# Segment sums of a graph network on one core: unread products on TensorE, VectorE's operands in PSUM

## The reference

```python
def _sage_conv(h, src, dst, W_self, W_neigh, b):
    msg_sum = jax.ops.segment_sum(h[src], dst, num_segments=N_NODES)
    deg = jax.ops.segment_sum(jnp.ones_like(dst, dtype=h.dtype), dst, num_segments=N_NODES)
    h_neigh = msg_sum / jnp.maximum(deg, 1.0)[:, None]
    return h @ W_self + h_neigh @ W_neigh + b          # three layers: sage0, sage1, sage2
...
    msg = xt[row] * alpha[..., None]                   # attention over incoming edges: gat
    out = jax.ops.segment_sum(msg, col, num_segments=n)
...
    def f(y):                                          # called four times: rk0 to rk3
        return jax.ops.segment_sum(y[src3] * e3, dst3, num_segments=N)
...
    msg = h_all[src, etypes] * norm                    # a matrix per relation: rel
    agg = jax.ops.segment_sum(msg, dst, num_segments=x.shape[0])
```

## Time and profile before

| | |
|---|---|
| Median of 3 runs | 21,753.78 us (21,741.98 to 21,762.46) |
| Profiled execution | 21,875.38 us, its span 21,873.6 us |
[...]
| Busy: PE, PEld, DVE, ACT, POOL | 47%, 33%, 29%, 12%, 65% of the span |

### The profile page before, as it was taken

One profiled execution on the slowest core, in us unless ns is written; L12 is line 12 of the kernel. 1 busy time (PEld: TensorE's weight loads), 2 busy tenths in 40 slices (PEclk: granted clock), 3 DMA queues, 4 the chain that ended last, 5 costly groups with the idle time before them and its releaser, 6 DMA issues.

```text
span 21873.6 us, 147184 instructions
## 1 busy us (share of the span) xinstructions
PE 10234.6 (47%) x41175; PEld 7163.9 (33%) x41176; DVE 6368.7 (29%) x12754; ACT 2697.4 (12%) x4406; POOL 14143.2 (65%) x14027
## 2 busy tenths in 40 slices
PE   5214444444477634434444444444444344448744
PEld 2113333333222323323333333333333333334333
DVE  8401111111477632222222222222222222226422
ACT  0001101010155421101000011001011001100010
POOL 5876676766755676676666666666666666660365
PEclk8655555555688755555555556555555565658855
DMA  1111211211100011121212112121211212125412
GB/s 31 9 23 46 46 42 46 42 46 47 13 1 1 2 14 46 46 48 46 45 47 43 51 46 46 46 48 46 46 47 46 48 46 46 46 46 211 188 46 45
DMA packets 555319, 1025.63 MB, mean 47 GB/s; under 512 B 276823, under 2 KB 344031, under 8 KB 529110
## 3 DMA queue, kind: packets, MB, share of 16 engines
q0 software_dynamic: 448640, 761.10, 16.4%
q1 hardware_dynamic: 102595, 256.61, 3.1%
q10 hardware_dynamic: 3600, 1.51, 0.0%
HBM read 767.92 MB, written 248.53 MB: 46 GB/s over the span
## 4 chain that ended last, share of the span: by engine, by line
POOL 35%; another core or an unknown queue 20%; issue 20%; PE 12%; DVE 7%; DMA 3%; ACT 2%; DVEq 1%; ACTq 0%; POOLq 0%; SPq 0%
POOL rows L405 28%; POOL list_f L389 5%; PE ps L1011 4%; PE ps L1101 3%; POOL list_r L389 3%; ACT work L462 2%; PE ps L1055 2%; DMA rows<-table,rows_F 1%; DVE onehot L701 1%; DVE rows L715 1%; DVE peak_tile L816 1%; DMA rows<-table,rows_R 1%; PE ps L1052 1%; PE ps L1017 0%
## 5 line engine op out<-in xcount | busy, mean ns | idle before, releaser
L1011 PE MATMUL ps<-rows,onehot 128*128 128x128 f32 (+1 forms) x22880 | 5352.9, 406 | 8395.6 <-DVE rows L715 4747.5
L405 POOL DMA_INDIRECT rows<-table,rows_F x7040 | 6864.8, 975 | 3332.5 <-issue 2028.8
L1011 PEld LDWEIGHTS ps<-rows,onehot 128*128 128x128 f32 x22880 | 4677.5, 299 | 9555.0 <-issue 7950.5
L405 POOL DMA_INDIRECT rows<-table,rows_R x3520 | 3419.8, 972 | 1630.1 <-issue 995.5
L462 ACT COPY work<-ps 128x1188 f32 x1430 | 1641.9, 1148 | 16874.2 <-remote 9132.3
L701 DVE TENSOR_TENSOR onehot<-iota,list_F 128x512 f32<-128x512 f32 x1980 | 1284.5, 690 | 5973.0 <-ACT work L462 3385.1
L1000 PE MATMUL ps<-naught 128*128 128x396 bf16 x4290 | 1592.9, 505 | 1492.3 <-issue 1491.9
L405 POOL DMA_INDIRECT rows<-rel_table,rows_F x880 | 851.6, 968 | 1261.1 <-DMA rel_table<-list_R 856.3
L389 POOL DMA_INDIRECT list_f<-list_F,work x850 | 1064.6, 1252 | 401.6 <-issue 258.7
L413 POOL DMA_INDIRECT rows<-peak_table,rows_F x880 | 831.3, 945 | 761.7 <-PE ps L1055 534.4
L389 POOL DMA_INDIRECT list_r<-list_R,rows_R x850 | 1110.6, 1307 | 259.0 <-issue 259.0
(11 more groups left out here) (198 smaller groups left out, 6211.3 us busy)
## 6 DMA issues: line engine op xcount, KB each, us to landing
rel_table<-list_R SPq DMA_DIRECT2D x196, 1024.0 KB, 3.9
rows<-table,rows_F POOLq DMA_INDIRECT x7040
rows<-table,rows_R POOLq DMA_INDIRECT x3520
table<-H SPq DMA_DIRECT2D x5, 3136.0 KB
rows<-peak_table,rows_F POOLq DMA_INDIRECT x880
rows<-rel_table,rows_F POOLq DMA_INDIRECT x880
list_f<-list_F,work POOLq DMA_INDIRECT x850
list_r<-list_R,rows_R POOLq DMA_INDIRECT x850
```

The source lines that it names most:

```text
L405: pool.indirect_dma_start(out=rows[:, t % UNROLL, 0:FEAT], out_offset=None, in_=from_table, in_offset=bass.IndirectOffsetOnAxis(ap=rows_of ...
L1011: ins = mm(into, onehot[:, s, :], rows[:, s, 0:width], start=False, stop=True, skip_group_check=True)
```

## The change

TensorE's two extra jobs in a window go to VectorE. `clear_half` writes the zeros by a memset, and `add_first` adds the running sums of the first block to the half in PSUM; ScalarE now waits for `window_added`, which add_first reports. VectorE's compare reads `iota_ps`, a copy of iota in PSUM bank 6, and its scaling reads the weights from the same bank, copied there for 96 tiles at a time. Behind each quad TensorE issues four products of the identity with itself, 128x512 in fp32, into bank 7, which nothing reads (`keep_clock`). In the unscaled passes TensorE waits for both membership matrices of a window at once.

```diff
+IDLE_PRODUCTS = 4
...
+CHUNK = (512 - P) // HEADS
...
+        iota_ps = ps[:, 6, 0:P]
+        weights_ps = ps[:, 6, P:]
...
+        def weights_of(name):
+            L = lists[name[-1]]
+            return share if name == "gat F" else L[:, :, 7:8] if name == "rel F" else L[:, :, 3:3 + HEADS]
...
-                    act.wait_ge(window_summed, m0 + w + 1)
+                    act.wait_ge(window_added, m0 + w + 1)
...
-            def block_sums(name, weights=None, aux=None):
-                L = lists[name[-1]]
+            def block_sums(name, aux=False):
+                key, L = name[-1], lists[name[-1]]
                 n0, m0 = quads_before(name), windows_before(name)
-                def members_of_window(w):
+                width = AUX if aux or name == "sage0 F" else FEAT
+                def clear_half(w):
                     if m0 + w >= 2:
                         dve.wait_ge(window_stored, m0 + w - 1)
+                    v.memset(half_of[w % 2][:, :, 0:SLOTS * AUX // SLOT_BANKS], 0.0)
+                def members_of_window(w):
                     for q in (2 * w, 2 * w + 1):
                         slots = slice(q % QRING * QUAD, (q % QRING + 1) * QUAD)
-                        v.tensor_tensor(onehot[:, slots, :], iota[:, :].unsqueeze(1).to_broadcast([P, QUAD, P]),
+                        v.tensor_tensor(onehot[:, slots, :], iota_ps.unsqueeze(1).to_broadcast([P, QUAD, P]),
                                         L[:, q * QUAD:(q + 1) * QUAD, 2].unsqueeze(2).to_broadcast([P, QUAD, P]),
                                         ALU.is_equal).then_inc(quad_members, 1)
                 def scale_quad(q):
-                    slots, tiles = slice(q % QRING * QUAD, (q % QRING + 1) * QUAD), slice(q * QUAD, (q + 1) * QUAD)
+                    at, words = q * QUAD % CHUNK, 1 if name == "rel F" else HEADS
+                    if at == 0:
+                        n = min(CHUNK, TILES - q * QUAD)
+                        if q:
+                            dve.wait_ge(quad_scaled, n0 - quads_before(SCALED[0]) + q)
+                        st(v.tensor_copy(weights_ps[:, 0:n * words].rearrange("p (t h) -> p t h", h=words), weights_of(name)[:, q * QUAD:q * QUAD + n, :]))
+                    weights = weights_ps[:, at * words:(at + QUAD) * words].rearrange("p (t h) -> p t h", h=words)
+                    slots = slice(q % QRING * QUAD, (q % QRING + 1) * QUAD)
                     dve.wait_ge(quad_landed[name][q % QRING], 16 * QUAD * (q // QRING + 1))
-                    if aux is not None:
-                        st(move(rows[:, slots, FEAT:AUX], aux[:, tiles, :]), False)
-                    at = rows[:, slots, 0:FEAT]
-                    if weights is None:
-                        v.tensor_tensor(at, at, L[:, tiles, 7].unsqueeze(2).to_broadcast([P, QUAD, FEAT]), ALU.mult).then_inc(quad_scaled, 1)
-                    else:
-                        at = at.rearrange("p t (h c) -> p t h c", c=HC)
-                        v.tensor_tensor(at, at, weights[:, tiles, :].unsqueeze(3).to_broadcast([P, QUAD, HEADS, HC]), ALU.mult).then_inc(quad_scaled, 1)
-                v.memset(SUM_OF[name[-1]][:, 0, :], 0.0).then_inc(sums_clear, 1)
+                    if aux:
+                        st(move(rows[:, slots, FEAT:AUX], weights), False)
+                    here = rows[:, slots, 0:FEAT].rearrange("p t (h c) -> p t h c", h=words)
+                    v.tensor_tensor(here, here, weights.unsqueeze(3).to_broadcast([P, QUAD, words, FEAT // words]), ALU.mult).then_inc(quad_scaled, 1)
+                firsts = []
+                def add_first(w):
+                    if w % 10 == 0:
+                        firsts[:] = firsts_of(mybir.EngineType.DVE, key, w, 10)
+                    dve.wait_ge(quad_summed, n0 + 2 * w + 2)
+                    if m0 + w:
+                        dve.wait_ge(window_stored, m0 + w)
+                    half = half_of[w % 2][:, 0, 0:width]
+                    v.tensor_tensor(half, half, sums_flat[key][:, bass.ds(firsts[w % 10], width)], ALU.add).then_inc(window_added, 1)
+                st(v.memset(SUM_OF[key][:, 0, :], 0.0))
+                st(v.tensor_copy(iota_ps, iota[:, :]))
+                clear_half(0)
                 members_of_window(0)
                 for w in range(WINDOWS):
                     if name in SCALED:
                         scale_quad(2 * w)
+                    if w:
+                        add_first(w - 1)
+                    if name not in SCALED and w + 1 < WINDOWS:
+                        clear_half(w + 1)
                     if w + 1 < WINDOWS:
                         members_of_window(w + 1)
                     if name in SCALED:
                         scale_quad(2 * w + 1)
+                        if w + 1 < WINDOWS:
+                            clear_half(w + 1)
+                add_first(WINDOWS - 1)
...
+            def keep_clock():
+                for _ in range(IDLE_PRODUCTS):
+                    mm(ps[:, 7, :].rearrange("p (a b) -> p a b", a=4), ident[:, :], ident[:, :].unsqueeze(1).to_broadcast([P, 4, P]), start=True, stop=True)
             def block_sums(name, width=FEAT):
-                key, n0, m0 = name[-1], quads_before(name), windows_before(name)
-                pe.wait_ge(sums_clear, SUMS.index(name) + 1)
+                key, n0 = name[-1], quads_before(name)
                 for w in range(WINDOWS):
-                    if w % 2 == 0:
-                        firsts = firsts_of(mybir.EngineType.PE, key, w, 2)
                     slots = slots_of(mybir.EngineType.PE, key, w)
                     half = half_of[w % 2].rearrange("p k f -> p (k f)")
-                    cleared = SLOTS * AUX // SLOT_BANKS
-                    for k in range(SLOT_BANKS):
-                        mm(half_of[w % 2][:, k, 0:cleared].rearrange("p (a b) -> p a b", a=4), naught[:, :],
-                           naught[:, 0:cleared // 4].unsqueeze(1).to_broadcast([P, 4, cleared // 4]), start=True, stop=True)
                     for j in range(WINDOW):
                         q, s = 2 * w + j // QUAD, (w * WINDOW + j) % UNROLL
                         if j % QUAD == 0:
                             if name in SCALED:
                                 pe.wait_ge(quad_scaled, n0 - quads_before(SCALED[0]) + q + 1)
                             else:
-                                pe.wait_ge(quad_members, n0 + q + 1)
+                                if j == 0:
+                                    pe.wait_ge(quad_members, n0 + q + 2)
                                 pe.wait_ge(quad_landed[name][q % QRING], 16 * QUAD * (q // QRING + 1))
                         into = half[:, 0:width] if j == 0 else half[:, bass.ds(slots[j - 1], width)]
                         ins = mm(into, onehot[:, s, :], rows[:, s, 0:width], start=False, stop=True, skip_group_check=True)
                         if j % QUAD == QUAD - 1:
                             ins.then_inc(quad_summed, 1)
-                    if m0 + w:
-                        pe.wait_ge(window_stored, m0 + w)
-                    mm(half[:, 0:width], ident[:, :], sums_flat[key][:, bass.ds(firsts[w % 2], width)],
-                       start=False, stop=True, skip_group_check=True).then_inc(window_summed, 1)
+                            keep_clock()
             def turn(dst_bank, of, j):
                 return tr(ps[:, dst_bank + j // 4, (j % 4) * P:(j % 4 + 1) * P], of, ident[:, :])
```

More of the change, by code:

```diff
@@ L553, in _ @@
             v.memset(zeros[:, :], 0.0).then_inc(consts, 1)
-            v.memset(naught[:, :], 0.0).then_inc(consts, 1)
             st(v.tensor_scalar(valid[:, :], part[:, :], float(LAST), None, ALU.is_lt), False)
@@ L860, in _ @@
             dve.wait_ge(shares_exp, ITERS + 1)
-            block_sums("gat F", weights=share, aux=share)
+            block_sums("gat F", aux=True)
             st(v.tensor_scalar(REC[:, :, :], ACC[:, :, FEAT:AUX], 1e-16, None, ALU.add))
@@ L882, in _ @@
                         name_rows("R", 0)
-                    attr = lists[key][:, :, 3:3 + HEADS]
-                    block_sums(f"rk{k} {key}", weights=attr, aux=attr if k == 0 else None)
+                    block_sums(f"rk{k} {key}", aux=k == 0)
                 n = AUX if k == 0 else FEAT
```

6 lines of the change are left out of this document (2 added, 4 removed).

## The result

The changed kernel took 21,860.72 us (median of 5 runs, 21,841.7 to 21,869.27), the kernel before 21,752.14 us (5 runs, 21,719.23 to 21,762.46). The ratio is 1.0051, with a 95% interval of 1.0036 to 1.0066: slower, by 108.6 us in the medians. The forecast of 19,730 us and its whole range were missed.

The account below looks back on a forecast made before the run. POOL's gathers were taken as the bound, with 2,051 us of excess from late completions and long gathers; 21,875 - 2,051 + 26 = 19,850, less 122 for plain runs, gave 19,730 us, range 19,620 to 20,450.

Parts of the forecast that it names:

- What bounds the kernel: Thirteen gather passes: POOL's undisturbed pitch is 1.248 us a gather, and the passes last 2,051 us longer than POOL needs.
- late completions: POOL's waits before gathers for TensorE and "remote": 1,687 us beyond ordinary issue gaps, with TensorE some 9 us late in one stretch.
- long gathers: Gathers in the passes running over 0.944 us, beginning under VectorE instructions that read two SBUF tensors: 335 us.
- unread products: Four TensorE products behind each quad keep the clock full and remove the late completions: 1,687 us, bounds 0 to 1,687.
- rival 2: Late completions stay, coming of something other than TensorE's idleness or clock: 21,417 us if all, 20,570 if half; chance 0.12.
- VectorE's operands in PSUM: Compares and scalings read one SBUF tensor instead of two, so long gathers end: 335 us taken, bounds 0 and 335.
- VectorE's new work: Clear, add, compares and scalings per window on VectorE: 4.5 us of a 9.98 us window, hidden under POOL.
- Clears and first block off TensorE: L1000 and L1017 leave TensorE; beside POOL's time, so worth nothing alone, but they make room for the products.
- The sum: Whole execution: 21,875 - 2,051 + 26 = 19,850 us, less 122 gives 19,730; everything outside the 13 passes stays.
- The correction of -122 us: Whole execution: the median of plain runs, 21,753.8 us, lies 121.6 us below the profiled one, so 122 is subtracted.
- the edges: Per pass, an iota copy, one clear and the last products: at most 3.45 us; 2 us allowed, 26 us in all.
- Rival 3: TensorE becomes the bound at every quad, slower than before, if the granted clock does not rise under the products; chance 0.05.

Follow-up runs that it names:

- chip C: Chip of the third group of follow-up runs; the kernel before takes 19,808 us there, and the changed kernel without products 19,671.43 us.
- chip D: Chip of the fourth group of follow-up runs; the kernel before takes 21,892 us there, and the changed kernel 22,016.21 us.
- paced: Changed kernel with a POOL IOTA behind each gather, waiting for the IOTA before it: 19,803.05 us (ratio 1.001) and 19,832.61 us (1.0012) on chips A and C.
- half-size kernels: Changed kernel gathering 64 rows instead of 128 (19,157.61 and 19,153.53 us), or 64 words a row instead of 128 (19,631.91 and 19,637.13), on chips A and C.
- chips A and C: Chips of the first and third groups of follow-up runs; the kernel before takes 19,784 and 19,808 us there.
- chip B: Chip of the second group of follow-up runs; the kernel before takes 21,907.84 us there, and the changed kernel 22,028.66 us.
- group 2: Runs on chip B: kernel before 21,907.84 us, changed kernel 22,028.66, changed kernel with operands in SBUF 22,166.67, kernel before with products alone 22,115.6.

## Why the prediction was wrong

*What bounds the kernel* was read rightly: POOL's gathers at 1.248 us, and an excess of 2,051 us made of late completions and long gathers. On chip C, where the late completions are missing, the passes do last 1,101 us.

*The step that failed* is the one on the unread products: "This part is what I expect to take the late completions away: they come with a mostly idle TensorE at the low clock". In the rows that is 561.28 of 1255 us busy at a granted 0.57. The step took a thing seen beside the waits for their cause. The evidence was a correlation within one trace, between stretches which differ in more than TensorE's activity: at L1101 no gather runs at all (POOL is busy 0.00 us in the earlier trace rows). Four cells now separate the two. Clock low and TensorE mostly idle (without products, the pass rk1 F): late on chip D (450.06 of 1249 us busy at a granted 0.51), on time on chip C (449.95 of 1101 at 0.50). Clock high and TensorE nearly full: late in the changed kernel (1063.73 of 1257 at 0.91, 2264.0 us remote), on time in the paced and the half-size kernels on chips A and C (90 to 94% busy at 0.99 to 1.00, no wait named remote). The late completions follow the chip, not the clock. The prediction's own sign for this step, waits of 4 us at a high clock, has come. Of the 1,687 us nothing was gained; rival 2's mechanism held whole. Its price, 21,417, was missed too, by 444 us: it still counted 335 us for the operands and nothing for the products. The lesson in the working is the 1,687 against its own lower bound of 0: the rows could not choose between the ends, and the forecast put 0.72 on the upper one.

*The products also cost*, which the sum had at nothing. Alone they cost 211.0 us on chip B; beside the rest of the change they cost 22,016.21 - 21,807.61 = 208.6 us on chip D. There POOL's waits for "remote" and TensorE are 2377.9 + 15.0 us with products and 2081.1 + 101.8 without, 210.0 apart, so the cost is waiting of POOL. On chip C, with completions on time, they cost nothing that shows. That they fit beside POOL was worked out rightly: a quad's products and sum take TensorE an estimated 3.45 + 0.86 = 4.31 us of POOL's 4.99 (from the earlier trace rows and 1.248 us a gather, as in group 2), and the quads in the timeline follow each other every 4.33 us (12136.48, 12140.81), at a granted 1.00 there. But the room was counted against a steady 4.99 us a quad. After each hold TensorE has queued quads to catch up on, and 3.6 us of products stand ahead of every one of them. In the kernel without products the 16 matmuls of two quads run in one go after a hold, in 3.94 us at a granted 0.55, 1.97 us a quad; with them each quad takes its 4.33. That this is how the 209 us arise is argued from the rows; no run tried a number of products between 0 and 4.

*VectorE's operands in PSUM* did what the prediction said to the gathers: 339.8 us of POOL time gone for the 335 forecast, and 810 back when the operands go back in the changed kernel. The term that failed is their worth in time: 335 was taken, and they are worth 138.0 and 140.3 us by the runs on chips B and D. On the chips with late completions part of POOL's saving is waited away again. On chips A and C the whole change without products gains 129 and 136 us, also far under 335; no trace of the kernel before was taken there, so how much of that is long gathers stays open. The longest gather is 986 ns with one SBUF operand in VectorE's compares and scalings, and 2667 ns with two (the kernel with SBUF operands on chip D, below, with one long gather under two compares). Which part of a gather is held, the runs do not tell.

```profile
1608.70 1.27 DVE L712 TENSOR_TENSOR onehot<-iota,list_F 128x512 f32<-128x512 f32 x2
1608.71 1.47 POOL L412 DMA_INDIRECT rows<-table,rows_F  x1 [0.30 <-issue]
```

```profile
L412 POOL DMA_INDIRECT rows<-table,rows_F x7040: 940/947/2667, 1482.1 to 18671.6; - x196
```

*VectorE's new work* was sized well or too high, and stayed hidden:

```profile
L741 DVE TENSOR_TENSOR ps<-ps,work 128x128 f32<-128x128 f32 (+1 forms) x1430 | 427.4, 299 | 7773.8 <-remote 7351.5
L729 DVE TENSOR_TENSOR rows<-rows,ps 128x512 f32<-128x512 f32 x2200 | 1495.2, 680 | 2025.1 <-DMA rows<-table,rows_F 876.8
L706 DVE MEMSET ps<- 128x1188 f32 x1430 | 1498.6, 1048 | 788.6 <-issue 498.5
```

The clear takes 1.05 us (1.40 taken, 1.0 the other end; the copy's row gives 1.33 in proportion, not 1.40), the add 0.30 (0.29), the scaling 0.68 (0.70). The 7,351.5 us that add_first waits for "remote" are the late completions again, now on VectorE.

*Clears and first block off TensorE*, together with the operands, are the rest. Without products the change is faster than before by 84 us on chip D (21,891.96 - 21,807.61) and by 129 to 136 us on chips A and C. Since the operands give 140.3 us on chip D, the moved clears and sums and the new waits would cost 56 us there, if the parts add up; that part was not run alone.

*The sum*, put right for chip D: operands -140, products +209, the rest +56 by difference, in all the measured +124. The correction of -122 us from profiled to plain time was also no property of the kernel: on chip B a profiled execution of before had a span of 21,891.5 us, below the 21,907.84 of its plain runs. The 3.45 us that bound the edges in the prediction are the estimate from the earlier trace rows given in group 2; no run had the edges alone.

Rival 3 (TensorE the bound for want of clock) did not happen: the granted 0.91 is above 4.31 / 4.99 = 0.86, the share at which TensorE's work on a quad would last as long as POOL's (an estimate, if that work goes with the clock). Nor did its sign, a TensorE without idle time and a wait of POOL at every quad: POOL waited for "remote" or TensorE before 854 of 11,440 gathers, and there are 2,860 quads.

What stays open is the cause of the late completions. It is not the clock, not TensorE's idleness, not the slot registers, not the gathers' rows. Nor do the gathered rows land late: VectorE's scaling starts 2.53 us after the start of the quad's last gather in the late stretch (12130.94, 12133.47) and on chip C alike (11021.03, 11023.56). The waits come in a rhythm. On chip D 715 gathers of the changed kernel wait for "remote" and 659 without products. POOL's waits of over 1.5 us for "remote" or TensorE stand there 23 us apart with products (679 of 811 distances), and without them most often 33 to 34 us (328 of 663). Where products are queued a wait ends in matmuls some 0.70 us apart. No row of the trace names what holds them. The unaltered changed kernel never ran on a chip with completions on time, and the kernel before was not traced on one, so that the chips differ by their completions is shown for the variants that ran on both kinds.

## What to carry to other kernels

A wait that the trace lays to "remote" has no cause in it; a forecast that rests on removing it should keep its price at both ends and give the lower end real weight, until an experiment has moved the wait. Filling TensorE to 86% of its period (an estimated 4.31 of 4.99 us a quad) was free on the chip where the work arrived evenly (passes of 1,100 us with products and half-width gathers, 1,101 without products), and cost some 210 us where it was held up: there, as argued above, the filler stands ahead of the catching up. And compare only with the kernel before on the same chip: here chips differed by 10%, twenty times the effect.

The version to keep is the changed kernel with IDLE_PRODUCTS = 0. It was faster than before on both kinds of chip: 0.9932 (0.9915 to 0.9948), 0.9931 (0.9915 to 0.9948) and 0.9968 (0.9956 to 0.9979).

## What the runs showed of the hardware

Chips of one type ran one program in two times: the kernel before at 19,784 and 19,808 us on two of them, and at 21,752 to 21,905 us in the other four results. For the kernel without products, traced on both kinds, 1,937 of the 2,136 us between chips D and C lie in the gather passes (16,262 and 14,325 us), and there in waits of POOL, on chip D 2081.1 us in 659, whose release the profile does not show. A gather of 64 rows took 908 ns against 944 for 128, so half the rows save 36 ns: nearly all of a gather's time on POOL did not go with its rows here. A VectorE operand in PSUM instead of SBUF changed the instruction's own time little (the compare took 678 to 680 ns at L712, 0.69 us before) and the time of POOL's gathers beside it a lot: the longest at L412 took 986 ns in the changed kernel and 2667 ns with both operands in SBUF, and all gathers of the passes together 10,821.99 and 11,618.63 us on chip D.
